# Attention kernel: eight of 48 row maxima between two sequences, splits in two pieces, norm and values in later steps

## The chip, the cores and the metric

The kernel runs on one core of a Trainium2 chip. The metric is the device time of one execution in microseconds (us), the median of several. Engines are named as in the profile: PE is TensorE (PEld its weight loads), DVE VectorE, ACT ScalarE, POOL GpSimd, SP the queue of SyncE, which here issues DMAs.

## What is computed

The reference is a small language model tower: embedding, a recurrent mixing block, a feed-forward block that contains an attention, a state space block and a mixture of experts. The change touches only the attention block, on a batch of 8 sequences (B) of 512 positions (T), width C = 192, 12 heads of 16:

```python
h = jnp.einsum('becd,fd->becf', xg, w1) + b1          # fc1: 768 hidden + 3 * 192 for q, k, v
x_mlp, x_qkv = (h[..., :MLP_HID], h[..., MLP_HID:])
attn = jax.nn.softmax(jnp.einsum('bhqd,bhkd->bhqk', q, k) * scale, axis=-1)
x_attn = jnp.einsum('bhqk,bhkd->bhqd', attn, v)
x_mlp = jax.nn.gelu(x_mlp, approximate=False)
y2 = jnp.concatenate([x_mlp, x_attn], axis=-1)
o = jnp.einsum('becf,of->beco', yg, w2) + b2
```

## The kernel before

The attention stage works through the sequences t = 0 to 7. For each there is a part `between(t)`, in which PE computes the six hidden tiles of the feed-forward (`mlp_tile`), and a part `turn(t)` of NS = 48 steps. A step n of a turn is written out by hand for each engine and does these things in this order:

- PE: one tile of transposed scores (`scores`, into `c_ps_s`), one tile of scores for a row maximum (`maxima`, into `c_ps_m`, for a tile that is LEAD = 20 ahead), in every fourth step the product with the values (`weigh`), and in fixed steps the work for other sequences: `y_transpose` and `qk` (query and key products) and `values` of sequence t + 1, and `out_part` (output projection) of t - 1, `max_transpose` and `att_transpose`.
- DVE: one row maximum (`row_maximum`, a reduction of 128x512 out of `c_ps_m`), and in fixed steps the split of queries and keys into three bf16 parts (`split_qk`, four operations), `norm_stats` and `norm_apply` of t + 2, `o_copy`, `v_copy`, `over_sum`, `negate_maxima`, `place_maxima`.
- ACT: one exponential (`exponent`, out of `c_ps_s`), the copies `att_copy` and, at the turn's start, `y_copy`; in `between` the Gelu of the hidden tiles.

The 48 tiles fall in three groups of 16 (GS), one for each four heads. The negated row maxima of a group enter the scores as a 97th row of the queries: `max_transpose` on PE, `place_maxima` on DVE, and a small DMA (`maxima_to_queries`) that must land ahead of step 16 for group 1, step 32 for group 2, and step 0 of the next turn for group 0.

Both `c_ps_m` and `c_ps_s` have two buffers. So `maxima` of tile n waits for the row maximum of tile n - 2, and `scores` of step n for the exponential of step n - 2. Every engine works in order: whatever stands ahead of a row maximum on DVE holds back PE. Other products share three banks of `c_ps_w` in the order that `work_order` lists.

The split queries and keys go to DRAM (`parts_to_scratch`) and come back as stacks of 96 rows in 12 DMAs for each group (`stacks_from_scratch`), on SP's queue. The stacks of a group of t + 1 can be read in only when the scores of that group of t are done.

```python
if n % GS == 0:
    pe.wait_ge(stack_in[n // GS], (t + 1) * STACK_LOADS * 16)
if t * NS + n >= 2:
    pe.wait_ge(m_read, t * NS + n - 1)
```

## Time and profile before

| | |
|---|---|
| time, median of 3 runs (lowest, highest) | 2247.56 us (2244.1, 2249.0) |
| time of the profiled execution | 2244.71 us |
| its span, from the first to the last instruction | 2243.0 us |
| mean granted clock of PE | 0.931 of full speed |
| PE busy | 1984.1 us (88%) |
| DVE busy | 1138.2 us (51%) |
| ACT busy | 752.2 us (34%) |
| POOL busy | 428.8 us (19%) |

The span and the time differ by 1.7 us, which lie outside the first and last instruction. The shares of busy time are means over stages with different limits. The attention stage lies between about 313 and 976 us of the span; what the change is worth must be read from the idle times of PE in it.

### The profile page before, as it was taken

The numbers are of one execution on the slowest core, as the hardware profiler recorded it, in microseconds if no ns is written. First come the engines' busy times: TensorE is split into PE (matmuls) and PEld (weight loads), VectorE is DVE, ScalarE is ACT, GpSimd is POOL, SyncE is SP. The second block draws the span as 40 slices with busy tenths as digits, with TensorE's granted clock in tenths as the row PEclk, the third lists the DMA queues.
The fourth block names the chain that finished last, engine by engine and source line by source line (L and its number), as shares of the span: only waits on it lengthen the run. The fifth ranks groups of instructions, "written<-read, shape, count | busy, mean of one in ns | idle before, by whom it ended". The sixth has DMA issues, their size and how long they took to land. (4 is left out here: it accounts for less than half of the span.)

```text
span 2243.0 us, 27883 instructions
## 1 busy us (share of the span) xinstructions
PE 1984.1 (88%) x10040; PEld 1248.4 (56%) x10048; DVE 1138.2 (51%) x2687; ACT 752.2 (34%) x1251; POOL 428.8 (19%) x526
## 2 busy tenths in 40 slices
PE   4996627989898999869999999779999999999997
PEld 2343412434344444345666666556556888888886
DVE  5898576566657555437766666245621222222221
ACT  2433002544454455536555555122111111111111
POOL 5200110022012100011111111010162222322222
PEclk9997558999999999969999999879999999999999
DMA  2600012111111111010000000020023312222321
GB/s 64 233 23 0 0 41 64 43 55 38 50 43 50 50 43 50 1 26 6 6 6 6 6 6 6 1 96 1 24 81 101 69 26 64 62 59 59 70 34 20
DMA packets 68618, 94.30 MB, mean 42 GB/s; under 512 B 15354, under 2 KB 57630, under 8 KB 66209
## 3 DMA queue, kind: packets, MB, share of 16 engines
q1 hardware_dynamic: 52354, 76.76, 10.7%
q0 software_dynamic: 16128, 15.76, 4.0%
q8 instruction: 81, 1.33, 0.2%
q14 instruction: 55, 0.45, 0.1%
HBM read 54.53 MB, written 39.47 MB: 42 GB/s over the span
## 5 line engine op out<-in xcount | busy, mean ns | idle before, releaser
L955 DVE TENSOR_REDUCE row_max<-c_ps_m 128x1 f32<-128x512 f32 x384 | 252.8, 686 | 153.4 <-PE c_ps_m L1104 149.2
L1270 ACT ACTIVATE e<-c_ps_s 128x512 f32<-128x512 f32 x384 | 218.1, 597 | 268.2 <-PE c_ps_s L1120 267.5
L2555 DVE TENSOR_TENSOR e_f<-e_ps_u,e_gate 128x512 f32<-128x512 f32 x120 | 83.0, 692 | 271.2 <-ACT e_gate L2837 178.8
L1104 PE MATMUL c_ps_m<-c_kT,qT 96*128 96x512 bf16 x384 | 152.9, 399 | 31.4 <-DVE row_max L955 30.7
L2356 POOL DMA_INDIRECT out<-m_o,m_row_of x80 | 125.7, 1571 | 283.2 <-issue 253.2
L1120 PE MATMUL c_ps_s<-qT,c_kT 97*128 97x512 bf16 x384 | 151.3, 397 | 31.1 <-DMA qT<-max_rows 20.3
L2772 PE MATMUL e_ps_o<-m_w,e_f 128*128 128x192 f32 x960 | 162.6, 326 | 0.9 <-DVE e_f L2555 0.9
L2772 PEld LDWEIGHTS e_ps_o<-m_w,e_f 128*128 128x128 f32 x960 | 158.1, 190 | 3.3 <-DVE e_f L2555 1.3
L2837 ACT ACTIVATE e_gate<-e_ps_g 128x512 f32<-128x512 f32 x120 | 71.6, 597 | 242.3 <-PE e_ps_g L2746 162.3
L2740 PE MATMUL e_ps_g<-m_xT,m_w 128*128 128x256 f32 x480 | 129.6, 392 | 1.0 <-DVE h L2387 1.0
L2740 PE MATMUL e_ps_u<-m_xT,m_w 128*128 128x256 f32 x480 | 123.2, 379 | 0.0
L2746 PE MATMUL e_ps_g<-m_xT,m_w 64*128 64x256 f32 x480 | 119.5, 389 | 0.0
L2750 PE MATMUL e_ps_u<-m_xT,m_w 64*128 64x256 f32 x480 | 119.5, 389 | 0.0
L1131 PE MATMUL c_ps_a<-e,v 128*32 128x512 f32 x768 | 108.2, 637 | 1.0 <-ACT e L1270 1.0
L2746 PEld LDWEIGHTS e_ps_g<-m_xT,m_w 64*128 64x128 f32 x480 | 85.0, 186 | 27.9 <-issue 19.9
L2740 PEld LDWEIGHTS e_ps_g<-m_xT,m_w 128*128 128x128 f32 x480 | 83.1, 190 | 28.4 <-issue 19.9
L1120 PEld LDWEIGHTS c_ps_s<-qT,c_kT 97*128 97x128 bf16 x384 | 37.5, 99 | 109.9 <-ACT e L1270 80.3
L2740 PEld LDWEIGHTS e_ps_u<-m_xT,m_w 128*128 128x128 f32 x480 | 91.2, 190 | 12.4
L2563 DVE TENSOR_SCALAR m_o<-e_ps_o,m_w_of 128x192 f32<-128x192 f32 x80 | 29.7, 413 | 126.1 <-PE e_ps_o L2772 126.1
L1094 PE MATMUL c_ps_w<-yT,w 96*128 96x512 f32 x192 | 90.9, 612 | 0.0
L1936 PE MATMUL d_ps_w<-d_y2T,wf 96*128 96x512 f32 x192 | 89.2, 611 | 0.9 <-ACT d_y2T L2005 0.9
L1104 PEld LDWEIGHTS c_ps_m<-c_kT,qT 96*128 96x128 bf16 x384 | 38.2, 100 | 91.3 <-DVE row_max L955 41.0
(430 smaller groups left out, 3798.2 us busy)
## 6 DMA issues: line engine op xcount, KB each, us to landing
dealt<-x SPq DMA_DIRECT2D x8, 1290.0 KB, 15.0
m_x<-dealt SPq DMA_DIRECT2D x40, 258.0 KB, 2.8
spread<-parts SPq DMA_DIRECT2D x24, 384.0 KB, 2.3
qT<-spread SPq DMA_DIRECT2D x144, 64.0 KB, 2.3
c_kT<-spread SPq DMA_DIRECT2D x144, 64.0 KB, 2.4
m_w<-in_w13e SPq DMA_DIRECT2D x8, 1152.0 KB, 5.2
m_w<-in_w2e SPq DMA_DIRECT2D x8, 576.0 KB, 6.3
out<-h SPq DMA_DIRECT2D x8, 384.0 KB, 4.6
```

What stands on the lines that cost most here:

```text
L955: dve.tensor_reduce(row_max[:, n // J, n % J:n % J + 1], ps_m[:, n % 2, :], AX_X, ALU.max)\
L1094: last = pe.matmul(bank(key), w1[0:CH + c, c, m * P:(m + 1) * P], yT[0:CH + c, c, :], start=c == 0, stop=c == 1)
L1104: pe.matmul(ps_m[:, n % 2, :], qT[0:STACK, h, j * P:(j + 1) * P], kT[0:STACK, h, :], start=True, stop=True).then_inc(m_psum, 1)
L1120: pe.matmul(ps_s[:, n % 2, :], kT[:, h, kc * P:(kc + 1) * P], qT[:, h, :], start=True, stop=True).then_inc(s_psum, 1)
L1131: last = pe.matmul(ps_a[32 * i:32 * i + 32, :], v[:, t % 2, kc, 4 * g + i, :], e[:, (4 * grp + i) % LIVE_E, :], start=kc == 0, stop=kc == ...
L1270: act.activation(e[:, n % LIVE_E, :], ps_s[:, n % 2, :], ACT.Exp, scale=QSCALE).then_inc(e_ready, 1)
L1936: last = pe.matmul(bank(key), wf1[:, c, col:col + P], y2T[:, c, :], start=c == 0, stop=c == 1)
L2356: pool.indirect_dma_start(out=out_rows, out_offset=bass.IndirectOffsetOnAxis(ap=row_of[:, n % 2, r:r + 1], axis=0), in_=o[:, n % 2, r, :], ...
L2740: last = pe.matmul(dst[:, q % 2, k, :], w13e[:, u, w, here[k]], xeT[:, b, 0, :], start=first and k == 0, stop=not first and k == 1, skip_g ...
L2746: g_last = pe.matmul(ps_ge[:, q % 2, k, :], w13e[0:HALF, u, 2, here[k]], xeT[0:HALF, b, 1, :], start=first and k == 0, stop=not first and ...
L2750: u_last = pe.matmul(ps_ue[:, q % 2, k, :], w13e[HALF:P, u, 2, here[k]], xeT[HALF:P, b, 1, :], start=first and k == 0, stop=not first and ...
L2772: last = pe.matmul(ps_oe[:, b, r, 0:C], fe[:, b, m, r * P:(r + 1) * P], w2e[:, u, m, :], start=m == 0, stop=m == IT - 1)
```

## The change

- In `between(t)` for t > 0 stand the matmuls and reductions of eight row maxima, tiles 20 to 27; a turn now starts with tile 28, and eight of its steps (4, 7, 11, 19, 22, 27, 30, 39) have none. Ahead of the first turn stand 28 maxima instead of 20.
- `split_qk` is cut in `split_high` (the first two operations, which free the bank) and `split_low` (the other two): steps 4, 7, 11 and 5, 9, 13 instead of both in 3, 6, 9. The third `qk` goes from step 9 to 10.
- `max_transpose` of groups 1 and 2 goes from steps 13 and 29 to 11 and 26, `place_maxima` to 12 and 27.
- `norm_stats` goes from step 8 to 19, `norm_apply` from 15 to 30, the values from 24 to 27 to steps 33, 35, 37 and 41, `o_copy` from 7 and 23 to 8 and 25, one `out_part` from 23 to 24.
- Ahead of the first turn the hidden tiles stand before the values, `place_maxima` stands ahead of the last ten row maxima, and SP reads the first stacks in before the third part is written out.

```diff
 LEAD = GS + 4
+BETWEEN = 8
+
+NO_MAXIMA = (4, 7, 11, 19, 22, 27, 30, 39)
+assert len(NO_MAXIMA) == BETWEEN
 BANKS = 3
 
 
+def maxima_of(n):
+
+    return [] if n in NO_MAXIMA else [LEAD + BETWEEN + n - sum(m < n for m in NO_MAXIMA)]
...
-            def split_qk(t, g):
+            def split_high(t, g):
...
                 dve.tensor_tensor(rest[:, :], qk, hml[:, 0, :], ALU.subtract).then_inc(w_by_dve, 1)
+
+            def split_low(g):
+
+                hml = parts[:, g]
...
             def between(t):
-                if t > 0:
-                    over_sum(t - 1, 2)
+                for n in range(LEAD, LEAD + BETWEEN):
+                    if n == LEAD + 2:
+                        over_sum(t - 1, 2)
+                    row_maximum(t, n)
 
             def turn(t):
                 prev, ahead = t > 0, t + 1 < B
                 for n in range(NS):
-                    to = n + LEAD
-                    if to < NS:
-                        row_maximum(t, to)
-                    elif ahead:
-                        row_maximum(t + 1, to - NS)
-                    if to == 2 * GS:
-                        negate_maxima(1)
-                    if to == 3 * GS:
-                        negate_maxima(2)
-                    if to == 4 * GS and ahead:
-                        negate_maxima(0)
-                    if ahead and n in (3, 6, 9):
-                        split_qk(t + 1, n // 3 - 1)
-                    if prev and n == 7:
+                    for to in maxima_of(n):
+                        if to < NS:
+                            row_maximum(t, to)
+                        elif ahead:
+                            row_maximum(t + 1, to - NS)
+                        if to == 2 * GS - 1:
+                            negate_maxima(1)
+                        if to == 3 * GS - 1:
+                            negate_maxima(2)
+                        if to == 4 * GS - 1 and ahead:
+                            negate_maxima(0)
+                    if ahead and n in (4, 7, 11):
+                        split_high(t + 1, (4, 7, 11).index(n))
+                    if ahead and n in (5, 9, 13):
+                        split_low((5, 9, 13).index(n))
+                    if prev and n == 8:
                         o_copy(t - 1, 0)
-                    if t + 2 < B and n == 8:
+                    if n == 12:
+                        place_maxima(t, 1)
+                    if t + 2 < B and n == 19:
                         norm_stats(t + 2)
-                    if n == 13:
-                        place_maxima(t, 1)
-                    if t + 2 < B and n == 15:
-                        norm_apply(t + 2)
                     if n == 22:
                         over_sum(t, 0)
-                    if prev and n == 23:
+                    if prev and n == 25:
                         o_copy(t - 1, 1)
-                    if ahead and 24 <= n < 28:
-                        v_copy(t + 1, n - 24)
-                    if n == 29:
+                    if n == 27:
                         place_maxima(t, 2)
+                    if t + 2 < B and n == 30:
+                        norm_apply(t + 2)
+                    if ahead and n in (33, 35, 37):
+                        v_copy(t + 1, (n - 33) // 2)
                     if n == 39:
                         over_sum(t, 1)
+                    if ahead and n == 41:
+                        v_copy(t + 1, 3)
                     if ahead and n == 45:
                         place_maxima(t + 1, 0)
...
                 v_copy(0, j)
-            for n in range(LEAD):
+            for n in range(LEAD + BETWEEN):
                 row_maximum(0, n)
-                if n == GS:
+                if n == GS - 1:
                     negate_maxima(0)
-            place_maxima(0, 0)
+                if n == GS + 1:
+                    place_maxima(0, 0)
             for t in range(B):
-                between(t)
+                if t > 0:
+                    between(t)
                 turn(t)
...
             def between(t):
-                prev = t > 0
+                first = iter(range(LEAD, LEAD + BETWEEN))
+
+                def row_maxima(count):
+                    for _ in range(count):
+                        maxima(t, next(first))
+
                 mlp_tile(t, 0)
-                if prev:
-                    weigh(t - 1, G3 * J - 1)
+                weigh(t - 1, G3 * J - 1)
                 mlp_tile(t, 1)
+                row_maxima(2)
                 mlp_tile(t, 2)
-                if prev:
-                    att_transpose(t - 1, 2)
+                att_transpose(t - 1, 2)
+                row_maxima(1)
                 mlp_tile(t, 3)
+                row_maxima(1)
                 mlp_tile(t, 4)
-                if prev:
-                    xa_transpose(t - 1, 0)
-                    xa_transpose(t - 1, 1)
+                row_maxima(1)
+                xa_transpose(t - 1, 0)
+                xa_transpose(t - 1, 1)
+                row_maxima(1)
                 mlp_tile(t, 5)
+                row_maxima(2)
 
             def turn(t):
                 prev, ahead = t > 0, t + 1 < B
                 for n in range(NS):
                     scores(t, n)
-                    to = n + LEAD
-                    if to < NS:
-                        maxima(t, to)
-                    elif ahead:
-                        maxima(t + 1, to - NS)
+                    for to in maxima_of(n):
+                        if to < NS:
+                            maxima(t, to)
+                        elif ahead:
+                            maxima(t + 1, to - NS)
                     if n % 4 == 1 and n > 4:
                         weigh(t, n // 4 - 1)
                     if ahead and n < 2:
                         y_transpose(t + 1, n)
                     if prev and n in (2, 4, 5, 7):
                         out_part(t - 1, 0, (2, 4, 5, 7).index(n))
-                    if ahead and n in (3, 6, 9):
+                    if ahead and n in (3, 6, 10):
                         qk(t + 1, n // 3 - 1)
-                    if n == 13:
+                    if n == 11:
                         max_transpose(t, 1)
-                    if prev and n in (18, 20, 21, 23):
-                        out_part(t - 1, 1, (18, 20, 21, 23).index(n))
+                    if prev and n in (18, 20, 21, 24):
+                        out_part(t - 1, 1, (18, 20, 21, 24).index(n))
                     if n == 22:
                         att_transpose(t, 0)
-                    if ahead and 24 <= n < 28:
-                        values(t + 1, n - 24)
-                    if n == 29:
+                    if n == 26:
                         max_transpose(t, 2)
+                    if ahead and n in (33, 35, 37):
+                        values(t + 1, (n - 33) // 2)
                     if n == 39:
                         att_transpose(t, 1)
+                    if ahead and n == 41:
+                        values(t + 1, 3)
                     if ahead and n == 45:
                         max_transpose(t + 1, 0)
...
             for g in range(G3):
                 qk(0, g)
+            for m in range(FC1_TILES):
+                mlp_tile(0, m)
             for j in range(J):
                 values(0, j)
-            between(0)
-            for n in range(LEAD):
+            for n in range(LEAD + BETWEEN):
                 maxima(0, n)
-            max_transpose(0, 0)
+                if n == GS + 1:
+                    max_transpose(0, 0)
...
-            for g in range(G3):
-                parts_to_scratch(0, g)
-            for g in range(G3):
-                stacks_from_scratch(0, g)
+            parts_to_scratch(0, 0)
+            parts_to_scratch(0, 1)
+            stacks_from_scratch(0, 0)
+            parts_to_scratch(0, 2)
+            stacks_from_scratch(0, 1)
+            stacks_from_scratch(0, 2)
             maxima_to_queries(0, 0)
             for t in range(B):
                 ahead = t + 1 < B
                 if ahead:
-                    for g in range(G3):
+                    for g in range(2):
                         parts_to_scratch(t + 1, g)
                 maxima_to_queries(t, 1)
                 if ahead:
+                    parts_to_scratch(t + 1, 2)
                     stacks_from_scratch(t + 1, 0)
```

DVE in a middle turn, from the second split on; `parts` and `rest` are the split's, `row_max` a row maximum, `o` is `o_copy`, `c_stats`, `c_mv` and `c_var_eps` are `norm_stats`. Before:

```order
L939 CAST parts<-c_ps_w 128x512
L941 TENSOR_TENSOR rest<-c_ps_w,parts 128x512
L943 CAST parts<-rest 128x512
L945 TENSOR_TENSOR parts<-rest,parts 128x512
L955 TENSOR_REDUCE row_max<-c_ps_m 128x1
L990 TENSOR_TENSOR o<-c_ps_w,b 128x384
L955 TENSOR_REDUCE row_max<-c_ps_m 128x1
L115 BN_STATS c_stats<-x 128x6 x4
L118 BN_AGGR c_mv<-c_stats 128x2 x4
L120 TENSOR_SCALAR c_var_eps<-c_mv 128x4
L955 TENSOR_REDUCE row_max<-c_ps_m 128x1
L939 CAST parts<-c_ps_w 128x512
```

Now, from the second split's first piece on, to `max_rows`, which is `place_maxima`:

```order
L952 CAST parts<-c_ps_w 128x512
L954 TENSOR_TENSOR rest<-c_ps_w,parts 128x512
L972 TENSOR_REDUCE row_max<-c_ps_m 128x1
L1007 TENSOR_TENSOR o<-c_ps_w,b 128x384
L972 TENSOR_REDUCE row_max<-c_ps_m 128x1
L960 CAST parts<-rest 128x512
L962 TENSOR_TENSOR parts<-rest,parts 128x512
L972 TENSOR_REDUCE row_max<-c_ps_m 128x1
L952 CAST parts<-c_ps_w 128x512
L954 TENSOR_TENSOR rest<-c_ps_w,parts 128x512
L972 TENSOR_REDUCE row_max<-c_ps_m 128x1
L985 CAST max_rows<-c_ps_w 16x128
```

Between two row maxima now stand at most two operations of a split; before it was four, and `norm_stats` stood in the same stretch.

PE between two sequences: L1094 are the hidden tiles, L1131 `weigh`, L1141 `att_transpose`, L1149 `xa_transpose`, L1120 the scores and L1104 the maxima. Before:

```order
L1094 MATMUL c_ps_w<-yT,w 128x512 x2
L1131 MATMUL c_ps_a<-e,v 32x512 x4
L1094 MATMUL c_ps_w<-yT,w 128x512 x4
L1141 MATMUL c_ps_w<-ident,att 128x128 x4
L1094 MATMUL c_ps_w<-yT,w 128x512 x4
L1149 MATMUL c_ps_w<-ident,xa 96x128 x8
L1094 MATMUL c_ps_w<-yT,w 128x512 x2
L1120 MATMUL c_ps_s<-qT,c_kT 128x512
L1104 MATMUL c_ps_m<-c_kT,qT 128x512
```

Now (L1120 are the hidden tiles, L1130 the maxima, L1157, L1167 and L1175 the others, L1146 the scores), from behind the second hidden tile to the turn's first scores, which follow:

```order
L1130 MATMUL c_ps_m<-c_kT,qT 128x512 x2
L1120 MATMUL c_ps_w<-yT,w 128x512 x2
L1167 MATMUL c_ps_w<-ident,att 128x128 x4
L1130 MATMUL c_ps_m<-c_kT,qT 128x512
L1120 MATMUL c_ps_w<-yT,w 128x512 x2
L1130 MATMUL c_ps_m<-c_kT,qT 128x512
L1120 MATMUL c_ps_w<-yT,w 128x512 x2
L1130 MATMUL c_ps_m<-c_kT,qT 128x512
L1175 MATMUL c_ps_w<-ident,xa 96x128 x8
L1130 MATMUL c_ps_m<-c_kT,qT 128x512
L1120 MATMUL c_ps_w<-yT,w 128x512 x2
L1130 MATMUL c_ps_m<-c_kT,qT 128x512 x2
```

Eight matmuls for maxima stand among the hidden tiles, the last two right ahead of the turn's first scores.

## Rows read from the trace of the kernel before

**Rows 1.** Windows by sequence: us; busy and (count) by engine; PEclk; DMA; GB/s

```profile
363.20:433.00 69.80, 60.54 (x276) 23.69 (x277) 45.89 (x98) 34.51 (x61) 6.44 (x8) 0.98 0.17 52
433.00:511.40 78.40, 71.52 (x340) 33.77 (x339) 47.42 (x100) 36.84 (x63) 11.94 (x14) 0.96 0.15 46
511.40:589.50 78.10, 71.56 (x340) 33.80 (x339) 47.30 (x100) 36.84 (x63) 11.94 (x14) 0.96 0.15 46
589.50:665.60 76.10, 68.65 (x341) 33.46 (x340) 47.20 (x100) 36.62 (x63) 11.94 (x14) 1.00 0.16 48
665.60:742.30 76.70, 70.15 (x340) 33.68 (x339) 47.25 (x100) 36.72 (x63) 11.94 (x14) 0.98 0.15 47
742.30:821.70 79.40, 72.82 (x340) 33.85 (x339) 47.33 (x100) 36.84 (x63) 13.70 (x15) 0.94 0.15 45
821.70:897.40 75.70, 68.59 (x340) 33.45 (x339) 44.54 (x87) 36.62 (x63) 5.50 (x6) 1.00 0.16 48
897.40:950.00 52.60, 45.49 (x243) 20.04 (x241) 22.56 (x44) 29.33 (x52) 5.50 (x6) 0.94 0.00 1
```

**Rows 2.** Waits from 363 to 950 us: total us, times, longest

```profile
PE c_ps_m L1104 <- DVE row_max L955: 27.3, 16, 2.7
PE c_ps_s L1120 <- DMA qT<-max_rows: 20.3, 17, 2.6
```

**Rows 3.** Timeline, PE, turn of sequence 3: start, us, instruction, [idle before]

```profile
592.27 0.39 PE L1120 MATMUL c_ps_s<-qT,c_kT 97*128 97x512 bf16 x1 [0.85 <-ACT e L1270]
...
606.60 0.39 PE L1104 MATMUL c_ps_m<-c_kT,qT 96*128 96x512 bf16 x1 [1.05 <-DVE row_max L955]
...
607.91 1.99 PE L1079 MATMUL c_ps_w<-yT,w 96*128 96x512 f32 x4
...
613.75 0.38 PE L1104 MATMUL c_ps_m<-c_kT,qT 96*128 96x512 bf16 x1 [2.55 <-DVE row_max L955]
...
618.04 0.38 PE L1120 MATMUL c_ps_s<-qT,c_kT 97*128 97x512 bf16 x1 [1.32 <-DMA qT<-max_rows]
...
639.40 0.38 PE L1120 MATMUL c_ps_s<-qT,c_kT 97*128 97x512 bf16 x1 [1.29 <-DMA qT<-max_rows]
...
640.36 1.07 PE L1131 MATMUL c_ps_a<-e,v 128*32 128x512 f32 x8
```

**Rows 4.** Timeline, DVE, the same turn

```profile
610.27 0.68 DVE L939 CAST parts<-c_ps_w 128x512 bf16<-128x512 f32 x1
...
612.92 1.94 DVE L955 TENSOR_REDUCE row_max<-c_ps_m 128x1 f32<-128x512 f32 x3
...
615.89 0.28 DVE L968 CAST max_rows<-c_ps_w 16x128 bf16<-16x128 f32 x1 [0.17 <-PE c_ps_w L1111]
```

**Rows 5.** Timeline, ACT, start of the same turn

```profile
590.33 1.28 ACT L1270 ACT_TABLE_LOAD   x1
591.62 0.60 ACT L1270 ACTIVATE e<-c_ps_s 128x512 f32<-128x512 f32 x1
```

**Rows 6.** Timeline, SP queue, first and last of six rows (12 issues)

```profile
652.97 1.46 SPq L853 DMA_DIRECT2D qT<-spread  x3
...
658.32 0.43 SPq L856 DMA_DIRECT2D c_kT<-spread  x1
```

**Rows 7.** Page, part 6: DMA issues, KB each, us to landing

```profile
qT<-spread SPq DMA_DIRECT2D x144, 64.0 KB, 2.3
```

**Rows 8.** Timeline, PE, ahead of the first turn

```profile
318.37 7.35 PE L1079 MATMUL c_ps_w<-yT,w 96*128 96x512 f32 x12 [0.69 <-ACT yT L1247]
...
334.71 12.80 PE L1094 MATMUL c_ps_w<-yT,w 96*128 96x512 f32 x24
347.34 0.60 PE L1104 MATMUL c_ps_m<-c_kT,qT 96*128 96x512 bf16 x2
...
363.22 0.61 PE L1120 MATMUL c_ps_s<-qT,c_kT 97*128 97x512 bf16 x1 [2.60 <-DMA qT<-max_rows]
```

**Rows 9.** Window of 4 us behind a wait of 2.56 us; columns as in Rows 1

```profile
689.00:693.00 4.00, 3.17 (x14) 0.75 (x15) 2.98 (x7) 0.60 (x1) 0.00 (x0) 0.74 0.25 98
```

More of the change, by code:

```diff
@@ L736 @@
 LEAD = GS + 4
+BETWEEN = 8
+NO_MAXIMA = (4, 7, 11, 19, 22, 27, 30, 39)
+assert len(NO_MAXIMA) == BETWEEN
 BANKS = 3
+def maxima_of(n):
+    return [] if n in NO_MAXIMA else [LEAD + BETWEEN + n - sum(m < n for m in NO_MAXIMA)]
 def work_order(by_end=False):
-    order = [("y", 0, c) for c in range(2)] + [("qk", 0, g) for g in range(G3)] + [("v", 0, j) for j in range(J)]
+    order = [("y", 0, c) for c in range(2)] + [("qk", 0, g) for g in range(G3)]
     for t in range(B + 1):
@@ L761, in work_order @@
         if not prev:
-            order.append(("mx", t, 0))
+            order += [("v", t, j) for j in range(J)] + [("mx", t, 0)]
         if ahead:
@@ L770, in work_order @@
             order += out[0:1] + qk + [("mx", t, 1)] + out[1:2] + [("at", t, 0)]
+        order.append(("mx", t, 2))
         if ahead:
-            order += [("v", t + 1, j) for j in range(J)]
-        order += [("mx", t, 2), ("at", t, 1)]
+            order += [("v", t + 1, j) for j in range(3)]
+        order.append(("at", t, 1))
         if ahead:
-            order.append(("mx", t + 1, 0))
+            order += [("v", t + 1, 3), ("mx", t + 1, 0)]
     return order
@@ L1040, in _ @@
             for g in range(G3):
[L1041 removed]
+                split_high(0, g)
+                split_low(g)
             norm_apply(1)
```

1 line of the change is left out of this document (removed).

## Prediction

> **What bounds the kernel now.** I read the windows by sequence first, to see which engine the attention stage waits on. In a middle sequence PE is busy 68.7 of 76.1 us, DVE 47.2, ACT 36.6 [rows 1]: PE is the bound, and only its idle time can be won, or lost. Next the waits of PE in this stage: 27.3 us behind row maxima on DVE, 20.3 us behind the small DMA that puts the maxima into the queries [rows 2]. Then the timeline of one turn, to see where they lie [rows 3]: 0.85 us at step 2 (exponential), 1.05 and 2.55 us at steps 9 and 12 (row maxima), 1.32 and 1.29 us at steps 16 and 32 (DMA). These five make 7.06 of the 7.45 us in which PE is idle in that sequence. Last the clock. The sequences with granted clock 1.00 take 76.1 and 75.7 us, mean 75.9; four others hold the same work and take 78.4, 78.1, 76.7 and 79.4, together 9.0 us more, at 0.96, 0.96, 0.98 and 0.94 [rows 1]. In each the clock had been full (2.4 GHz) until the long row-maximum wait, here one of 2.56 us, and was partly at 1.2 GHz in the next window: mean 0.74 [rows 9]. So these waits cost more than their own length.
>
> **Why PE waits there.** A split is four operations, from 610.27 to the next reduction at 612.92: 2.65 us [rows 4]. The reductions themselves follow one another every (1.94 - 0.69) / 2 = 0.62 us. A step with nothing but scores and a maximum is two matmuls 0.22 us apart (two take 0.60, one 0.38) [rows 8], so 0.44 us: PE runs ahead of DVE in bare steps by 0.18 us each, and a split, with `norm_stats` in front of the third, empties both buffers.
>
> **The change part by part.**
>
> *Eight maxima in between.* The same 48 matmuls and reductions are done for a sequence, so nothing is saved by count. PE's between part grows by 8 x 0.22 = 1.7 us and its turn shrinks by the same. DVE's turn loses 8 x 0.62 = 5.0 us, and this work falls where DVE had only `over_sum`. What pays is that DVE keeps up. One new wait arises at the turn's start: the last two maxima of between, two scores and the next maximum come within 0.9 us, but the third of these maxima needs the reduction of the first, 0.41 us behind it plus 0.74 until PE may refill the buffer; I charge 0.5 us. The step-2 wait of 0.85 us shrinks: two maxima and that 0.5 us now stand between the last hidden tile and step 2, 0.94 in all, so it is gone. The table load of 1.28 us and the exponential at 591.62 right behind it set this wait [rows 5]; they start at the last hidden tile as before.
>
> The Trainium skill, "ScalarE: Activation LUTs", section What ACT_TABLE_LOAD costs, puts a switch of tables at about 2.66 us, a load and a drain of 1.38. By that price the exponential would come 1.38 us behind the load, step 2 would still wait some 1.3 us in each of seven turns, and the sum below would be 9 us smaller. The trace disagrees: the exponential starts 0.01 us behind the load [rows 5].
>
> *Splits in halves, three steps without a maximum beside them, `norm_stats` away.* I walked through steps 3 to 17 with the durations of the rows. The first two splits lie beside output parts and query-key products (1.99 us [rows 3]), and the halves of about 1.5 and 1.2 us end before PE needs the buffer: waits 1.05 and 2.55 go. The third is the tight one. Its product ends in step 10; then DVE has 1.5 us (high half), 0.62 (a row maximum) and 0.28 (`place_maxima`), and from the start of that copy at 615.89 to the scores at 618.04 it was 2.15 us [rows 3, 4]: 4.3 us from the end of the product. PE has in that time steps 11 to 15: nine matmuls at 0.22, a `weigh` of 1.07 plus 0.1, and a transposition of 0.12, 3.3 us. It waits 0.9 us at step 16 on the DMA. The low half, 1.2 us, then stands in front of the reductions of steps 14 to 17, which costs some 1.1 us more over steps 13 to 17. So 3.6 + 1.32 us go, and 2.0 come back.
>
> *`max_transpose` of group 2 in step 26.* Six steps ahead of step 32 with a `weigh` among them are over 3 us for a chain of 2.5 us: the 1.29 us go. Bare steps follow at the pace of ACT, and I charge 0.3 us.
>
> *Values in steps 33, 35, 37, 41; `norm_apply` in 30; bank order.* The same work; at step 35 it fills a gap that PE leaves to ACT. I put it at 0. If that cover is missing it costs at most the 0.3 us of the four gaps each.
>
> *SP's order.* The stacks of heads 0 to 3 are now due in step 25 instead of 28, those of heads 8 to 11 in step 5 instead of 12. One set is issued from 652.97 to 658.75 and lands 2.3 us later [rows 6, 7]: 8.1 us. The last set starts at the turn's end, here 652.97; the next turn began at 665.6 [rows 1], with the eight maxima 1.7 us later, and steps 0 to 4 hold at least 5 us: due after 19.3 us, 11 us of slack. The first set waits for the third low half and the write-out behind it and is due, in my walk, some 12 us after them, 3 us of slack. Neither costs anything; in the shorter first turn it may be half a us.
>
> *Ahead of the first turn.* Before, values waited for bank after bank while DVE split, and only at 334.71 came 12.80 us of hidden tiles, then the first maximum at 347.34 [rows 8]. The query-key products ended at 325.7. Hidden tiles can follow at once, each when a split's high half has freed a bank, one every 2.65 us. A tile has the shape of a query-key product, 1.99 us with its tail [rows 3], so 1.8 behind another: the third ends at 325.7 + 2 x 2.65 + 1.8 = 332.8, the other three take 5.4 us, and the values, estimated by their 192 columns of 512, 4 x 1.8 x 0.375 = 2.7: first maximum at 340.9, 6.4 us earlier. Then 28 instead of 20: the 20 took (363.22 - 347.34 - 2.60) / 20 = 0.66 us each, so 5.3 us more. The DMA's 2.60 us [rows 8] lie under the last ten. First scores 6.4 + 2.6 - 5.3 = 3.7 us earlier, and the first turn has 1.7 us less of matmuls. Of these 5.4 us, 2.6 are in the DMA total below, so 2.8 are counted here.
>
> **The sum.** To be removed: 27.3 + 20.3 us of [rows 2], and the step-2 waits, 0.85 in seven turns, 6.0: 53.6 us. Put back, per turn 0.5 + 0.9 + 1.1 + 0.3 = 2.8, less 0.5 of small stalls behind `over_sum` and of the last steps: 2.3, in eight turns 18.4 us. Net 35.2. The clock's 9.0 us come on top, since no single wait above 0.94 us is left; the start gives 2.8. Total 47 us. The profiled execution took 2244.7 us (span 2243.0 and 1.7 around it), so 2197.7; it was at the low end of the three runs with a median of 2247.6, but what spreads the runs is probably the clock's falls, which go. I forecast **2198 us**, 2.2% less. Later stages stay as they are.
>
> **The rivals.**
>
> *A. The waits only move.* DVE is in order and has 47 us of work in a sequence, most of it in the turn. If the halves hit the reductions wherever they stand, the row-maximum waits come back for the most part: of 35 us net only the DMA's part stays, 20.3 - 8 x 0.9 = 13, and half of the clock's: 13 + 4.5 + 2.8 = 20 us, 2224 us. For it speaks that step 11 to 17 is tight by my own walk; against it that DVE's share over the whole turn is now about 41 of 57 us.
>
> *B. The clock falls all the same.* Then its 9.0 us are not won, and if it falls in the other four turns too, another 4 x 2.2 = 9 are lost: 47 - 18 = 29 us, 2216 us. For it: some 2 us of idle time within 5 us remain in steps 13 to 17. Against it: the sequence from 589.5, with 1.05 and 2.55 us of waits, kept a clock of 1.00 [rows 1, 3], so it takes at least that much. The Trainium skill, "TensorE: Matmul & The Clock Gate", section What's actually happening, says that the half rate is the default and activity releases it; by that rule fewer idle stretches mean fewer falls, which agrees with [rows 9].
>
> *C. Slower.* The stacks of heads 8 to 11 come too late for step 5. PE would stand in each of seven turns, with scores and values queued behind the maximum and ACT behind them. It decides from the point where each turn loses the 47 / 7 = 7 us that are won; with 11 us of slack the set would have to take 18 us longer than 8.1. At 20 us longer, 9 lost in each turn: 2244.7 - 47 + 63 = 2261 us. Nothing in the trace speaks for it.
>
> **How the numbers follow.** Forecast 0.76, A 0.11, B 0.09, C 0.02, and 0.02 for no change within 0.2% (4.5 us), about what a measurement of this kernel can tell. The forecast's own range: nothing put back at all gives 65 us (2179), put back twice as much gives 29 us (2216). I cut the fast end, which needs every wait to vanish: 2182. At the slow end the range takes in B and leaves out most of A: 2219. Faster by over 0.2%: 0.76 + 0.11 + 0.09 = 0.96, of which I give 0.02 away for what I have not seen; same 0.03; slower 0.03.
>
> **What would show it.** PE's wait for row maxima down from 27.3 to under 12 us, for the DMA from 20.3 to under 9; sequences of 70 to 72 us, all at a clock of 1.00; the first scores near 359.5 instead of 363.2. Wrong would make it: row-maximum waits of over 1 us in steps 12 to 17, a clock under 1.00 in the middle sequences, or a wait of the first maximum of a group for its stack.

## The result, and the profile after

| | before | after |
|---|---|---|
| time, median (lowest, highest; runs) | 2246.76 us (2244.1, 2249.0; 4) | 2194.63 us (2192.55, 2197.47; 4) |
| ratio, 95% interval | | 0.9761 [0.9743, 0.9779] |
| span of the profiled execution | 2243.0 us | 2190.8 us |
| mean granted clock of PE | 0.931 | 0.936 |
| PE, DVE, ACT, POOL busy | 1984.1, 1138.2, 752.2, 428.8 us | 1974.5, 1137.2, 750.8, 428.5 us |

The medians differ by 52.1 us, 2.3%; by the ratio in the table it is 2.4%. DVE, ACT and POOL do the same work in the same time.

Windows by sequence of the kernel after, columns as in [rows 1]:

```profile
361.16:425.50 64.34, 61.58 (x274) 23.39 (x273) 45.43 (x98) 34.71 (x61) 6.44 (x8) 0.94 0.18 56
425.50:497.90 72.40, 70.34 (x341) 33.90 (x339) 47.20 (x100) 36.60 (x63) 11.90 (x14) 0.98 0.16 50
497.90:568.60 70.70, 68.64 (x340) 33.24 (x339) 47.21 (x100) 36.61 (x63) 11.89 (x14) 1.00 0.17 51
568.60:641.00 72.40, 70.34 (x341) 34.16 (x339) 47.30 (x100) 36.60 (x63) 11.89 (x14) 0.98 0.17 50
641.00:713.30 72.30, 70.24 (x340) 33.59 (x339) 47.31 (x100) 36.61 (x63) 11.91 (x14) 0.98 0.16 50
713.30:784.00 70.70, 68.64 (x340) 33.24 (x339) 47.20 (x100) 36.60 (x63) 13.67 (x15) 1.00 0.17 51
784.00:856.40 72.40, 70.34 (x341) 33.79 (x339) 44.55 (x87) 36.61 (x63) 5.51 (x6) 0.98 0.16 50
856.40:910.00 53.60, 45.94 (x260) 21.40 (x259) 18.90 (x43) 30.87 (x55) 5.52 (x6) 1.00 0.00 1
```

Only two lengths are left among the six middle sequences (the second to the seventh row): 70.7 us where the clock is 1.00, 72.4 where it is 0.98. PE is busy for 68.6 us at full clock, as before [rows 1], and idle for 2.06 us (70.70 - 68.64), where it was 6.5 to 7.5. The waits of PE from 355 to 905 us (total us, times, longest), beside [rows 2]:

```profile
PE c_ps_m L1130 <- DVE row_max L972: 7.9, 19, 0.7
PE c_ps_s L1146 <- ACT e L1308: 5.0, 14, 0.6
PE c_ps_s L1146 <- DMA qT<-max_rows: 4.4, 8, 0.7
```

The same stretch of before, 355 to 960 us, gives 28.5, 10.1 and 20.3 us. None of these waits is longer than 0.73 us now; the one longer wait in the stretch, 0.96 us for an exponential, stands ahead of the last `weigh`. The timeline of PE in one turn, all waits over 0.2 us, beside [rows 3]:

```profile
499.32 0.39 PE L1130 MATMUL c_ps_m<-c_kT,qT 96*128 96x512 bf16 x1 [0.35 <-DVE row_max L972]
...
521.44 0.38 PE L1146 MATMUL c_ps_s<-qT,c_kT 97*128 97x512 bf16 x1 [0.58 <-DMA qT<-max_rows]
522.36 0.39 PE L1130 MATMUL c_ps_m<-c_kT,qT 96*128 96x512 bf16 x1 [0.54 <-DVE row_max L972]
...
539.50 0.39 PE L1146 MATMUL c_ps_s<-qT,c_kT 97*128 97x512 bf16 x1 [0.26 <-ACT e L1308]
```

They stand where they were forecast, at steps 0, 16, 16 and 32. That at step 2 is gone though the table load and the exponential stand as before (timeline of ACT, same turn):

```profile
498.96 1.28 ACT L1308 ACT_TABLE_LOAD   x1
500.26 0.60 ACT L1308 ACTIVATE e<-c_ps_s 128x512 f32<-128x512 f32 x1
```

The pair at step 16 comes from DVE. Its timeline: `max_rows` is placed at 519.32, and then one reduction, the third low half and four reductions follow in a row:

```profile
519.32 0.27 DVE L985 CAST max_rows<-c_ps_w 16x128 bf16<-16x128 f32 x1
...
520.50 0.43 DVE L960 CAST parts<-rest 128x512 bf16<-128x512 f32 x1
521.00 0.69 DVE L962 TENSOR_TENSOR parts<-rest,parts 128x512 bf16<-128x512 f32 x1
521.61 2.48 DVE L972 TENSOR_REDUCE row_max<-c_ps_m 128x1 f32<-128x512 f32 x4
```

Every middle sequence has such a pair of 1.12 us in all, and behind it the clock falls in four of the six; it does not behind the pair shown above. Two windows of 4 us from one with a fall; its pair, 0.55 and 0.57 us, ends at 593.08, and in the window ahead the clock was 1.00, columns as in [rows 1]:

```profile
592.00:596.00 4.00, 3.29 (x14) 0.69 (x15) 2.82 (x5) 1.19 (x2) 0.00 (x0) 0.80 0.53 171
596.00:600.00 4.00, 4.00 (x19) 3.58 (x18) 3.07 (x11) 2.17 (x4) 0.73 (x1) 0.77 0.47 125
```

Ahead of the first turn, timeline of PE, beside [rows 8]: first query-key product, first maximum, first scores, which wait for nothing now:

```profile
320.96 7.30 PE L1105 MATMUL c_ps_w<-yT,w 96*128 96x512 f32 x12 [0.69 <-ACT yT L1285]
...
342.74 0.60 PE L1130 MATMUL c_ps_m<-c_kT,qT 96*128 96x512 bf16 x2
...
361.16 0.63 PE L1146 MATMUL c_ps_s<-qT,c_kT 97*128 97x512 bf16 x1
```

**Where the 52 us come from.** I cut the trace of every kernel, one execution each, in the same way: the attention stage runs from the first query-key product to the end of the last output projection, and its sequences are parted by the Gelu table loads.

| us | before | after | difference |
|---|---|---|---|
| first query-key product to first scores | 44.85 | 40.20 | -4.65 |
| first turn | 57.52 | 51.14 | -6.4 |
| six middle sequences, sum | 464.4 | 430.9 | -33.6 |
| last sequence and tail | 83.65 | 76.43 | -7.2 |
| attention stage | 650.5 | 598.6 | -51.8 |
| ahead of it, behind it | 318.4, 1274.2 | 321.0, 1271.2 | +2.6, -3.0 |

What lies ahead starts the stage anywhere from 317.9 to 323.8 us in the kernels below, whatever the edit, so I put the last row down to scatter.

### The profile page after: what moved, and what is told of

Same layout as the page of the kernel before. It is cut to its first block and busy times, and to the rows that moved or that the text cites. A ratio compares the mean times of both kernels' runs of the same rounds, so it can differ in the third digit from the quotient of the medians.

```text
span 2190.8 us, 27883 instructions
## 1 busy us (share of the span) xinstructions
PE 1974.5 (90%) x10040; PEld 1243.3 (57%) x10048; DVE 1137.2 (52%) x2687; ACT 750.8 (34%) x1251; POOL 428.5 (20%) x526
## 5 line engine op out<-in xcount | busy, mean ns | idle before, releaser
L1130 PE MATMUL c_ps_m<-c_kT,qT 96*128 96x512 bf16 x384 | 150.3, 398 | 11.0 <-DVE row_max L972 10.9
L1146 PE MATMUL c_ps_s<-qT,c_kT 97*128 97x512 bf16 x384 | 145.5, 389 | 12.3 <-ACT e L1308 5.0
L1157 PE MATMUL c_ps_a<-e,v 128*32 128x512 f32 x768 | 105.9, 625 | 1.0 <-ACT e L1308 1.0
L1146 PEld LDWEIGHTS c_ps_s<-qT,c_kT 97*128 97x128 bf16 x384 | 36.5, 98 | 106.7 <-ACT e L1308 82.0
L1120 PE MATMUL c_ps_w<-yT,w 96*128 96x512 f32 x192 | 90.8, 597 | 1.2 <-DVE rest L954 1.2
L2368 POOL DMA_INDIRECT dealt<-e_x,slot x64 | 62.4, 975 | 121.1 <-issue 115.7
```

The lines of the kernel that those rows point to most:

```text
L1120: last = pe.matmul(bank(key), w1[0:CH + c, c, m * P:(m + 1) * P], yT[0:CH + c, c, :], start=c == 0, stop=c == 1)
L1130: pe.matmul(ps_m[:, n % 2, :], qT[0:STACK, h, j * P:(j + 1) * P], kT[0:STACK, h, :], start=True, stop=True).then_inc(m_psum, 1)
L1146: pe.matmul(ps_s[:, n % 2, :], kT[:, h, kc * P:(kc + 1) * P], qT[:, h, :], start=True, stop=True).then_inc(s_psum, 1)
L1157: last = pe.matmul(ps_a[32 * i:32 * i + 32, :], v[:, t % 2, kc, 4 * g + i, :], e[:, (4 * grp + i) % LIVE_E, :], start=kc == 0, stop=kc == ...
```

## The experiments

The kernels ran on three chips (four kernels each). On the second and third, what lies behind the attention stage takes 1298 to 1313 us in these traces instead of 1271 to 1275, and the kernel before takes 2273.55 and 2282.61 us instead of 2247.05. The stage itself takes as long: the unedited change gave 598.6 us on the third chip as in the trace of the section above, whose chip isn't on record and whose times are those of the first. So times are compared as ratios to the kernel before on the same chip, and stages across chips. A stage is one execution, and one fall of the clock more or less moves it by 1.65 us, so differences of 3 to 4 us between stages say little by themselves.

| kernel | median us | ratio [95% interval] | stage us | middle sequences us |
|---|---|---|---|---|
| first chip: before | 2247.05 | | 650.5 | 75.7 to 79.4 |
| `e_between_only` | 2249.75 | 1.0011 [1.0000, 1.0023] | 653.5 | 73.7 to 80.0 |
| `e_no_between` | 2237.91 | 0.9961 [0.9945, 0.9978] | 643.0 | 76.0 to 79.0 |
| `e_late_max` | 2226.6 | 0.9906 [0.9890, 0.9923] | 629.3 | 73.0 to 78.2 |
| `e_whole_splits` | 2199.25 | 0.9782 [0.9766, 0.9799] | 602.2 | 71.3 to 72.9 |
| second chip: `e_norm_back` | 2236.46 | 0.9834 [0.9786, 0.9882] | 608.4 | 70.7 to 74.1 |
| `e_values_back` | 2220.25 | 0.9762 [0.9719, 0.9805] | 595.0 | 70.8 to 72.4 |
| `e_start_old` | 2229.89 | 0.9819 [0.9766, 0.9871] | 604.3 | 70.7 to 72.4 |
| `e_place_early` | 2225.75 | 0.9774 [0.9730, 0.9817] | 598.3 | 70.8 to 72.4 |
| third chip: `e_change_again` | 2225.86 | 0.9757 [0.9730, 0.9783] | 598.6 | 70.7 to 72.4 |
| `e_place_first` | 2238.98 | 0.9811 [0.9777, 0.9846] | 605.1 | 71.9 to 73.5 |
| `e_early_skip14` | 2221.19 | 0.9744 [0.9714, 0.9774] | 592.0 | 70.4 |
| `e_early_low18` | 2220.74 | 0.9726 [0.9697, 0.9754] | 588.0 | 69.5 |

The diffs below are against the change, `e_between_only` against the kernel before.

### The eight maxima alone, and all but them

**`e_between_only`**: `LEAD`, `maxima_of` and `between` of the change put into the kernel before; splits, norm, values and transpositions stay.

```diff
+NO_MAXIMA = (4, 7, 11, 19, 22, 27, 30, 39)
 def between(t):
-    over_sum(t - 1, 2)
+    for n in range(LEAD, LEAD + BETWEEN):
+        if n == LEAD + 2:
+            over_sum(t - 1, 2)
+        row_maximum(t, n)
```

> The kernel before with only the eight maxima between the sequences and the eight steps without one; splits whole in steps 3, 6, 9, norm, values, transpositions of maxima and the start as before. Theory (the gain is made of separate waits of PE, each removed by its own edit): the waits of 1.05 us at step 9 and part of the 2.55 us at step 12 go, 0.5 us comes at the turn's start, the two DMA waits of 1.3 us stay, the long wait stays above 1.5 us and the clock still falls behind it: 8 to 16 us won, 2231 to 2239 us. Rival (relief of DVE by eight reductions is what pays): most of the 52 us are there, under 2210 us.

It gained nothing, 1.0011. Timeline of PE in a middle turn:

```profile
544.67 0.61 PE L1115 MATMUL c_ps_m<-c_kT,qT 96*128 96x512 bf16 x1 [2.64 <-DVE row_max L963]
...
549.59 0.59 PE L1131 MATMUL c_ps_s<-qT,c_kT 97*128 97x512 bf16 x1 [0.43 <-DMA qT<-max_rows]
...
572.43 0.38 PE L1131 MATMUL c_ps_s<-qT,c_kT 97*128 97x512 bf16 x1 [1.49 <-DMA qT<-max_rows]
```

The wait of 1.05 us [rows 3] is gone, since step 7, right behind the second split, has no maximum, but the long one of 2.64 us is still there: the third split is four operations, with `norm_stats` ahead of them, and no gap of one maximum covers that. The clock falls behind it, columns as in [rows 1]:

```profile
545.00:549.00 4.00, 4.00 (x14) 0.78 (x13) 1.83 (x4) 0.82 (x2) 0.00 (x0) 0.50 0.21 83
```

At step 16 the DMA's wait is down to 0.43 us, as I read it only because PE goes at half clock up to there. Both theories missed. PE's idle time in the six middle sequences did go down, from 41.1 to 35.0 us, but they take 464.9 us instead of 464.4: the clock, below 1.00 in five of the six where it was four, took it back. Lead in the maxima alone, with the splits whole, is worth nothing.

**`e_no_between`**: the change without the eight; since a group's maxima are then ready later (those of group 1 in step 11 instead of 3, those of group 2 in step 27 instead of 24), transposition and placing go back to steps 13 and 29. Shown are the hunks for group 1.

```diff
-BETWEEN = 8
+BETWEEN = 0
-NO_MAXIMA = (4, 7, 11, 19, 22, 27, 30, 39)
+NO_MAXIMA = ()
-if n == 11:
+if n == 13:
     max_transpose(t, 1)
-if n == 12:
+if n == 13:
     place_maxima(t, 1)
...
```

> The changed kernel without the eight maxima between the sequences: every step has its maximum with a lead of 20, transpositions of maxima back in steps 13 and 29 (their inputs come later), the rest as changed. Theory: halves and the moved norm keep the row-maximum waits under 1.5 us, but both DMA waits of 1.3 us are back in eight turns (20 us) and DVE has 5 us more in a turn: 2213 to 2228 us. Rival (the eight maxima pay for nearly all): above 2235 us.

It was slower than I expected and as slow as the rival said, 0.9961. But row maxima aren't the reason: PE waits for them only 5.6 us from 355 to 960 us, 0.8 at most. The DMA's waits grew instead, to 33.6 us (timeline of PE, one turn):

```profile
588.79 0.39 PE L1143 MATMUL c_ps_s<-qT,c_kT 97*128 97x512 bf16 x1 [0.85 <-ACT e L1304]
...
609.02 0.39 PE L1127 MATMUL c_ps_m<-c_kT,qT 96*128 96x512 bf16 x1 [0.44 <-DVE row_max L972]
...
612.85 0.38 PE L1143 MATMUL c_ps_s<-qT,c_kT 97*128 97x512 bf16 x1 [2.84 <-DMA qT<-max_rows]
...
633.59 0.38 PE L1143 MATMUL c_ps_s<-qT,c_kT 97*128 97x512 bf16 x1 [1.31 <-DMA qT<-max_rows]
```

The DMA's wait at step 16 is longer than before the change (1.32 us [rows 3]), and the edit itself has a part in it: in step 13 `max_rows` now stands behind the third low half, though the last maxima of the group were negated 4 us earlier (timeline of DVE):

```profile
606.80 0.17 DVE L977 TENSOR_SCALAR neg_max<-row_max 128x16 f32<-128x16 f32 x1
...
610.76 0.27 DVE L985 CAST max_rows<-c_ps_w 16x128 bf16<-16x128 f32 x1
```

So the rest of the change takes away the row-maximum waits without the eight. Alone, the eight make the stage 3.0 us longer and the rest makes it 7.5 us shorter; together, with the earlier placing, they give 51.8.

**`e_late_max`**: the change, eight included, but transposition and placing at steps 13 and 29 (the last two hunks above).

> The changed kernel with the transposition and placing of the maxima back in steps 13 and 29. Theory: DMA waits come back, about 1.3 us at step 32 and at step 16 more than before the change, some 2 us, because place_maxima now stands behind the low half of the third split in step 13; eight turns: 20 to 28 us lost, 2214 to 2224 us, clock falls in all middle sequences. Rival (ACT or DVE bind there anyway): under 2200 us.

Time and stage (629.3) are a little above what was expected; the clock is below 1.00 in five of the six middle sequences. That makes a staircase: before 650.5, all but the eight and the earlier placing 643.0, with the eight 629.3, with the earlier transposition and placing 598.6. The last edit, four step numbers, is the largest. Part of it is the order on DVE (timeline of DVE, then of PE):

```profile
602.67 0.43 DVE L960 CAST parts<-rest 128x512 bf16<-128x512 f32 x1
603.17 0.69 DVE L962 TENSOR_TENSOR parts<-rest,parts 128x512 bf16<-128x512 f32 x1
603.78 0.27 DVE L985 CAST max_rows<-c_ps_w 16x128 bf16<-16x128 f32 x1
```

```profile
605.87 0.38 PE L1146 MATMUL c_ps_s<-qT,c_kT 97*128 97x512 bf16 x1 [2.47 <-DMA qT<-max_rows]
...
624.38 0.38 PE L1146 MATMUL c_ps_s<-qT,c_kT 97*128 97x512 bf16 x1 [1.52 <-DMA qT<-max_rows]
```

At step 13 `max_rows` is placed behind the third low half, which takes 603.78 - 602.67 = 1.11 us, and the scores start 2.09 us behind it.

**`e_place_first`** takes this apart: late as `e_late_max`, but in step 13 placed ahead of the low half. The diff shows this order alone.

```diff
 if ahead and n in (4, 7, 11):
     split_high(t + 1, (4, 7, 11).index(n))
+if n == 13:
+    place_maxima(t, 1)
 if ahead and n in (5, 9, 13):
     split_low((5, 9, 13).index(n))
```

> The changed kernel with the maxima transposed in steps 13 and 29 (as before the change), but placed in step 13 ahead of the low half of the third split. Theory: of the 30.7 us that the late transposition cost the attention stage, the 1.2 us of the low half in front of the placing made some 10 in eight turns; the waits for the DMA fall from 31.6 to about 22 us and the time is 18 to 22 us above that of the changed kernel. Rival (the place of the transposition alone makes the loss): 28 us or more above it.

The wait at step 16 is 1.27 us instead of 2.47, as much as the low half takes:

```profile
593.31 0.38 PE L1146 MATMUL c_ps_s<-qT,c_kT 97*128 97x512 bf16 x1 [1.27 <-DMA qT<-max_rows]
```

Stage 605.1: this one order on DVE is worth 24 of the 30.7 us between `e_late_max` and the change, and the earlier steps 6.5. The ratios, 0.9906, 0.9811 and 0.9757, say some 21 and 12 us of 2247. The DMA's waits are 8.1 of them (31.6 us in the stage of the one, 23.5 in that of the other). Most of the rest is the clock: by windows it is 0.93 to 0.98 in five of six middle sequences of `e_late_max`, and below 1.00 in one of `e_place_first`. At full clock a middle sequence takes 73.0 us in `e_late_max`, 71.9 in `e_place_first` and 70.7 in the change: there the order and the earlier steps are worth about as much, and the earlier steps take away more of the DMA's waits (23.5 to 4.4 us). That the order has the larger share of the 30.7 us rests on how often the clock fell in one execution of each, five, one and four times. The expectation was right on the waits (22 us) and missed the time, and so did its rival: the kernel is 13.1 us above the change in the medians of its chip (6.5 in the stage), not 18 to 22, since it had left out what the clock gives back.

This order needs none of the eight maxima: without them the last maximum of group 1 is reduced in step 11, ahead of a transposition in step 13. `e_no_between` with `place_maxima` ahead of the low half was not run, so what the eight are worth with the good order is not known. With the bad one they are worth 13.7 us (643.0 against 629.3).

### The other parts, one at a time

**`e_whole_splits`**: the low half right behind the high half.

```diff
-if ahead and n in (5, 9, 13):
-    split_low((5, 9, 13).index(n))
+if ahead and n in (4, 7, 11):
+    split_low((4, 7, 11).index(n))
```

> The changed kernel with both halves of a split together in steps 4, 7 and 11. Theory: the third split holds place_maxima back by 1.2 us more, so the wait at step 16 grows from 0.55 to about 1.7 us in eight turns, and the wait for row maxima behind it goes from 0.57 to near 0: net 0.7 to 1.2 us a turn, 2199 to 2206 us. Rival (steps without maxima beside the splits are enough, halves give nothing): 2193 to 2197 us.

The time is as expected (stage +3.6), the way isn't. A sequence at full clock takes 71.3 us instead of 70.7, but one of the six has a fall instead of four; the stage is longer by the first turn (+1.8 us) and the last part (+2.9). The DMA's wait stays as it was; in place of the 0.54 us at the end of step 16 stand two waits ahead of it:

```profile
595.03 0.39 PE L1130 MATMUL c_ps_m<-c_kT,qT 96*128 96x512 bf16 x1 [0.61 <-DVE row_max L972]
...
596.04 0.39 PE L1130 MATMUL c_ps_m<-c_kT,qT 96*128 96x512 bf16 x1 [0.41 <-DVE row_max L972]
596.98 0.38 PE L1146 MATMUL c_ps_s<-qT,c_kT 97*128 97x512 bf16 x1 [0.55 <-DMA qT<-max_rows]
```

**`e_norm_back`**: `norm_stats` to step 8, `norm_apply` to 15.

```diff
-if t + 2 < B and n == 19:
+if t + 2 < B and n == 8:
     norm_stats(t + 2)
-if t + 2 < B and n == 30:
+if t + 2 < B and n == 15:
     norm_apply(t + 2)
```

> The changed kernel with norm_stats in step 8 and norm_apply in step 15 as before. Theory: 1.75 us of DVE work ahead of the third split and 1.24 us behind the placing make row-maximum waits in steps 9 to 17 longer by 1 to 2 us in six turns, with more falls of the clock: 2202 to 2212 us. Rival (DVE has the room): 2193 to 2197 us.

Stage +9.8 us, as expected. A sequence at full clock takes 72.7 us instead of 70.7; more falls of the clock did not come, it is two of six. The waits around the third split:

```profile
594.37 0.39 PE L1130 MATMUL c_ps_m<-c_kT,qT 96*128 96x512 bf16 x1 [0.76 <-DVE row_max L972]
...
596.33 0.39 PE L1130 MATMUL c_ps_m<-c_kT,qT 96*128 96x512 bf16 x1 [0.25 <-DVE row_max L972]
...
597.34 0.39 PE L1130 MATMUL c_ps_m<-c_kT,qT 96*128 96x512 bf16 x1 [0.41 <-DVE row_max L972]
598.28 0.38 PE L1146 MATMUL c_ps_s<-qT,c_kT 97*128 97x512 bf16 x1 [0.55 <-DMA qT<-max_rows]
599.23 0.39 PE L1130 MATMUL c_ps_m<-c_kT,qT 96*128 96x512 bf16 x1 [0.57 <-DVE row_max L972]
```

The pair at the end is the change's; 0.76, 0.25 and 0.41 stand ahead of it. `norm_stats` fills the slack that the halves have made.

**`e_values_back`**: values in steps 24 to 27, `o_copy` and the last output part in 23, bank order to match.

```diff
-if ahead and n in (33, 35, 37):
-    values(t + 1, (n - 33) // 2)
+if ahead and 24 <= n < 28:
+    values(t + 1, n - 24)
...
```

> The changed kernel with the values of the next sequence back in steps 24 to 27 (and the last output part and its copy back in 23). Theory: the same PE work, which fills fewer gaps: 0 to 1 us in each of seven turns, 2194 to 2202 us. Rival (values in late steps are what fills the pace of ACT there): above 2204 us.

A sequence without a fall takes 70.77 us against 70.72 of the change: moving the values is worth nothing that counts. The stage is 3.6 us shorter than the change's, but by fewer falls of the clock (two for four, 3.3 us), not by a wait.

**`e_start_old`**: ahead of the first turn values before hidden tiles, placing behind the last maximum, all parts written out before the first stack.

```diff
-for m in range(FC1_TILES):
-    mlp_tile(0, m)
 for j in range(J):
     values(0, j)
+for m in range(FC1_TILES):
+    mlp_tile(0, m)
...
```

> The changed kernel with the start as before: values ahead of the hidden tiles, the maxima of group 0 transposed and placed behind all 28, stacks read in only behind all three write-outs. Theory: the first maximum is 7 us later and the DMA wait of 2.6 us is back; the first scores come some 9 to 10 us later: 2203 to 2205 us. Rival (the stacks, not PE, set the start): under 2199 us.

The first scores come 50.06 us behind the first query-key product instead of 40.20, 9.86 us later, as expected. It shows that the new order of the start is worth 9.9 us. By the timelines 7.1 of them go to the hidden tiles (first maximum at 28.86 instead of 21.78) and 2.8 to the DMA under the last maxima; the order on SP was not tried by itself. The stage is longer by 5.7 only: two falls instead of four in the middle, and a first turn of 50.17 instead of 51.14.

**`e_change_again`**: the change unedited, on the third chip.

> The changed kernel once more, unedited, beside the next three on one chip. Both theories of the clock (it falls wherever some 1.1 us of waits stand in steps 15 to 17; or by chance, with the same waits) give 0.976 of the kernel before; sequences at a clock of 1.00 again 70.7 us and those with a fall 72.3 to 72.4, in the first case the same four of six, in the second another number of them.

Stage 598.60 against 598.63, again four falls in six sequences, but in other ones: 1, 3, 5 and 6 instead of 1, 3, 4 and 6. The waits are the same, so they alone don't decide; neither theory had the same number in other places.

### Better than the change

**`e_place_early`**: group 1 transposed in step 9 and placed in 10, ahead of the third split's product, bank order to match.

```diff
-if n == 12:
+if n == 10:
     place_maxima(t, 1)
-if n == 11:
+if n == 9:
     max_transpose(t, 1)
```

> The changed kernel with the maxima of group 1 transposed in step 9 and placed in step 10, ahead of the third query-key product and its split. Theory: the DMA wait of 0.55 us at step 16 goes, the row-maximum wait behind it (0.57 us) stays or grows by some 0.2 us as DVE is still behind; with less idle time at once the clock falls more seldom than in four of six middle sequences (1.65 us each): 3 to 11 us won, 2184 to 2192 us. Rival (the row-maximum wait takes its place in full, the clock falls as before): 2193 to 2196 us.

The rival held on the wait, and the time is the change's (0.9774 against 0.9761); the clock fell in two of six, not four, but the last part of the stage is 4.1 us longer. The DMA's wait is gone from the turn and its time is paid behind a row maximum (timeline of PE, then of DVE):

```profile
517.76 0.39 PE L1130 MATMUL c_ps_m<-c_kT,qT 96*128 96x512 bf16 x1 [1.18 <-DVE row_max L972]
```

```profile
515.91 0.43 DVE L960 CAST parts<-rest 128x512 bf16<-128x512 f32 x1
516.41 0.69 DVE L962 TENSOR_TENSOR parts<-rest,parts 128x512 bf16<-128x512 f32 x1
517.02 2.48 DVE L972 TENSOR_REDUCE row_max<-c_ps_m 128x1 f32<-128x512 f32 x4
```

The pair 0.58 + 0.54 of the change is now one wait of 1.18 us. What delays PE there is the amount of DVE's work in steps 11 to 16, as the next two kernels bear out, and the DMA only showed it first.

**`e_early_skip14`** (`NO_MAXIMA` has 14 in place of 19, on top of `e_place_early`), **`e_early_low18`** (third low half in step 18 instead, on top of `e_place_early`, and its write-out on SP behind the first stacks of t + 1):

```diff
-if ahead and n in (5, 9, 13):
-    split_low((5, 9, 13).index(n))
+if ahead and n in (5, 9, 18):
+    split_low((5, 9, 18).index(n))
```

```diff
 if ahead:
-    parts_to_scratch(t + 1, 2)
     stacks_from_scratch(t + 1, 0)
+    parts_to_scratch(t + 1, 2)
 maxima_to_queries(t, 2)
```

> The maxima of group 1 transposed in step 9 and placed in 10 (which alone turned the wait for the DMA into one of 1.18 us for a row maximum in step 16), and the step without a maximum moved from 19 to 14. Theory (DVE is late by what stands in steps 11 to 15): one reduction of 0.62 us less there leaves a wait of some 0.6 us; a sequence at full clock takes 70.2 instead of 70.8 us; with the start and the last turn 4 to 6 us under the changed kernel, more if the clock falls more seldom. Rival (the wait only moves to steps 19 to 21 behind norm_stats, which has lost its cover): no change.

> The maxima of group 1 transposed in step 9 and placed in 10, and the low half of the third split moved from step 13 to 18, where PE has output parts; on SP the third write-out stands behind the first read-in. Theory: 1.2 us of DVE work leave the tight place, the row-maximum wait of 1.18 us goes for the most part, idle time of PE in a sequence from 2.2 to about 1.2 us, sequences of 69.7 us with no fall of the clock: 10 to 15 us under the changed kernel (7 without the clock's part). Rival (the wait moves to steps 18 to 21, or the stacks come late in step 25): within 3 us of it.

Six sequences of 70.4 us for the first, in which the wait is down to 0.70 us, and of 69.5 for the second, in which PE is idle for 1.05 us. What is left of waits over 0.2 us in a turn of `e_early_low18`:

```profile
567.83 0.39 PE L1130 MATMUL c_ps_m<-c_kT,qT 96*128 96x512 bf16 x1 [0.35 <-DVE row_max L972]
...
586.75 0.39 PE L1146 MATMUL c_ps_s<-qT,c_kT 97*128 97x512 bf16 x1 [0.26 <-ACT e L1308]
...
606.83 0.39 PE L1146 MATMUL c_ps_s<-qT,c_kT 97*128 97x512 bf16 x1 [0.26 <-ACT e L1308]
```

No middle sequence has a fall. Its stage is 10.6 us shorter than the change's on the same chip, though the last part grew from 76.4 to 80.5 us, as it did in `e_place_early`; there the clock falls at the end (columns as in [rows 1]):

```profile
892.00:896.00 4.00, 2.24 (x14) 0.93 (x13) 0.88 (x5) 0.60 (x1) 0.00 (x0) 0.75 0.00 0
896.00:900.00 4.00, 3.32 (x14) 2.84 (x13) 0.00 (x0) 1.18 (x2) 0.00 (x0) 0.50 0.00 0
```

By time it is 2220.7 us against 2225.9 of the change, 0.9726 [0.9697, 0.9754] against 0.9757 [0.9730, 0.9783]. The intervals overlap, so that it is faster, by 5 us in the medians, is likely and not shown by the times; the shorter stage is shown by one trace of each. Expected were 10 to 15 us for it, which only the stage reaches, and 4 to 6 for `e_early_skip14`, which is 4.7 us under the change in the medians and 6.6 in the stage.

## Why the prediction was right, step by step

Forecast 2198 us, range 2182 to 2219; measured 2194.6.

- **PE is bound, and only its waits can be won: right.** 51.8 of the 52.1 us are in the attention stage, and busy times changed by nothing but the clock.
- **Which waits go, and what is put back: right in place, a little too dear.** Forecast per turn 0.5, 0.9, 1.1 and 0.3 us; measured 0.35, 0.58, 0.54 and 0.26. (By its own terms, 4.27 less 3.27 us, the second should have been 1.0.) A middle sequence at full clock went from 75.9 to 70.7 us: six times 5.2 are 31.2 us.
- **Step 2: right.** The exponential still starts 0.02 us behind the table load (498.96 + 1.28 to 500.26), and PE doesn't wait for it. By the price that the Trainium skill gives in "ScalarE: Activation LUTs", section What ACT_TABLE_LOAD costs, the forecast would have been 9 us higher, further from the result.
- **"The clock's 9.0 us come on top, since no single wait above 0.94 us is left": wrong.** This is the step that failed, and a clock under 1.00 in middle sequences was one of the signs that I had named. These sequences lost 9.0 us to the clock before and lose 6.6 now (4 x 1.65), so 2.4 are won. PE's idle time in a sequence went from 6.5 to 7.5 us down to 2.06, and still four of six have a fall, as before; each costs 1.65 us instead of 2.25 (9.0 / 4). That is rival B's reason at about a third of its price of 18 us. My argument against B, a sequence that had kept its clock with waits of 1.05 and 2.55 us, did not bear: what one sequence gets through, the next need not. The first turn, which the sum left out of the clock, got worse: its clock is 0.94 now, where it was 0.98 [rows 1].
- **What starts a fall stays open.** All middle sequences of the change have the same 1.12 us of waits at step 16, and four of six fell, on another chip others. `e_early_skip14` and `e_early_low18` have no such pair and no fall. But the same pair gave two falls in `e_values_back` and `e_start_old`, and with more idle time there were fewer: two in `e_norm_back` (3.5 us in a sequence), one in `e_whole_splits` (2.5 us), one in `e_place_first` (3.7 us or more, with waits of 1.3 and 1.5 us in each). So that the pair is the cause is not shown.
- **The error was balanced by terms set too low, which is luck.** Of the 47 us forecast, six eighths of the net 35.2 lay in the middle sequences, some 26, with 9 of clock on top, and some 12 in the rest; measured were 31.2, 2.4 and 18.25 (4.65 + 6.4 + 7.2). In the last part the clock had been at 0.94 [rows 1] and is now at 1.00, which my sum left out, and the start gave 4.65 us where 3.7 were forecast.
- **"What pays is that DVE keeps up": misread.** The eight maxima alone gave nothing, and without them the row-maximum waits were gone as well. The largest part, 30.7 us of the 51.8 (the change against `e_late_max`), is where the maxima of a group are transposed and placed, and 24 of these, the larger part of them clock, are that `place_maxima` stands ahead of the third low half. I had counted these DMA waits (20.3 us), and my walk had the right order, but as a by-product of the splits. What the eight add is 13.7 us under the late placing, and they make the steps 11 and 26 possible, 6.5 us; under the good order their worth is not measured.
- **Values at 0, SP's order at 0, norm away from the third split: right.** `e_values_back` 0.05 us for a sequence, `e_norm_back` +9.8 us. In the change's trace PE waits for no stack; in the first turn of four other kernels it stands 0.4 to 1.1 us for one (1.12 in `e_early_skip14`), where the prediction allowed for half a us.
- **Rivals.** A didn't come: row-maximum waits are 7.9 us, not most of 27.3. C didn't come.

## What to carry to other kernels

In a pipeline whose engines work in order, try an edit that gains lead and the edits that could use it apart and together: here the same lead gave nothing with whole splits and 13.7 us with the rest of the change. Place the small operation that starts a DMA (here 0.27 us, 2.1 us from there to its reader) ahead of any long one on its engine: 1.1 us of order cost 24 us of the stage in eight turns, 8 as waits and most of the rest as clock, which varies from execution to execution. And when a wait for a transfer is removed, look at what the same engine has to do in the steps around it: here the wait only changed its name.

## What the hardware showed

- PE's granted clock can fall behind idle time that is spread over two short waits: in the two windows of 4 us at and behind a pair of 0.55 and 0.57 us it was 0.80 and 0.77 of full speed, at a cost of 1.65 us. It doesn't do so each time. The same program on the same data had its falls in other sequences on another chip. The sequences of the change without a fall agree within 0.02 us in both traces.
- Behind a single wait of 2.64 us the next window of 4 us was at the half rate (0.50, the level of 1.2 GHz), while the kernel before kept its full clock in a sequence with one of 2.55 us [rows 1, 3].
- A small DMA reaches its reader 2.1 us behind the start of the cast that feeds it (519.32 to 521.44; 603.78 to 605.87).
- On two other chips the kernel before took 26.5 and 35.6 us longer, and in the traces the part behind the attention stage was longer and the stage was not (598.63 and 598.60 us). A difference of 5 us between kernels has to be taken from one chip.
